# Moving one batch's rounding ahead of the first attention slots, and context and weight pieces from VectorE to GpSimd

## The reference

```python
def _fp8_linear_pertensor(x, wq, w_scale, in_scale):
    xq = _div_clamp_fp8(x, in_scale)          # divide, clip to 448, bf16, round to fp8
    return einsum('bsi,oi->bso', xq * in_scale, wq) * w_scale
...
ln_out = _ln(hidden_states, ln_w, ln_b)
q  = _ln(_fp8_linear_pertensor(ln_out, wq, ...))    # 16 heads of 128, 8 groups of 2
k  = _ln(_fp8_linear_pertensor(ln_out, wk, ...));  v = _fp8_linear_pertensor(ln_out, wv, ...)
core = _gqa(q, k, v)                                # softmax attention
qx = _ln(_fp8_linear_pertensor(ln_out, wqx, ...))
kx, vx = split(einsum('bsi,oi->bso', cond, w_kv_x))   # cond: the context, not rounded to fp8
xout = _gqa(qx, _ln(kx), vx)
cat = _div_clamp_fp8(concatenate([core, xout]), proj_smooth)
x = x + einsum('bsi,oi->bso', cat, wproj) * scales
x = x + _ffn(_layernorm(x))                         # gate, up, silu, down
```

## Time and profile before

| | |
|---|---|
| median of 3 runs | 1735.4 us |
| the profiled execution | 1738.57 us, span 1736.7 us |
| PE / PEld busy | 1632.1 us (94%) / 1228.0 us (71%) |
| DVE / ACT / POOL busy | 1410.2 (81%) / 1359.8 (78%) / 1089.6 us (63%) |
| chain that ended last | PE 71%, DVE 9%, ACT 7%, issue 5%, POOL 4% |
| busiest POOL group | L1131, 512 x 1166 ns, idle before it 296.3 us |

### The profile page before, as it was taken

One profiled execution on the slowest core, in us unless ns is written; L12 is line 12 of the kernel. 1 busy time (PEld: TensorE's weight loads), 2 busy tenths in 40 slices (PEclk: granted clock), 3 DMA queues, 4 the chain that ended last, 5 costly groups with the idle time before them and its releaser, 6 DMA issues.

```text
span 1736.7 us, 43799 instructions
## 1 busy us (share of the span) xinstructions
PE 1632.1 (94%) x15491; PEld 1228.0 (71%) x15776; DVE 1410.2 (81%) x3228; ACT 1359.8 (78%) x2908; POOL 1089.6 (63%) x1031
## 2 busy tenths in 40 slices
PE   1569999999999999999999999999999899999999
PEld 1447778888888888888888888888888544444444
DVE  8999999999999999999999999998779763323232
ACT  6978999999999999999999999999999622222221
POOL 1357777777787777777777777778777613121211
PEclk9969999999999999999999999999999999999999
DMA  5947788887888888788878887888999980303000
GB/s 177 223 111 127 140 154 144 148 153 147 148 149 156 147 145 152 147 148 146 151 147 149 148 159 147 145 140 151 188 187 187 196 244 22 138 8 142 4 24 25
DMA packets 663603, 241.45 MB, mean 139 GB/s; under 512 B 619488, under 2 KB 636000, under 8 KB 662880
## 3 DMA queue, kind: packets, MB, share of 16 engines
q1 hardware_dynamic: 662096, 230.20, 68.1%
q0 software_dynamic: 1296, 8.52, 2.4%
HBM read 75.15 MB, written 29.51 MB: 60 GB/s over the span
## 4 chain that ended last, share of the span: by engine, by line
PE 71%; DVE 9%; ACT 7%; issue 5%; POOL 4%; SPq 3%; DMA 2%; DVEq 0%; ACTq 0%; POOLq 0%
PE ps_pj L673 21%; PE ps_s L739 6%; PE ps_o L722 5%; PE ps_o L724 5%; PE ps_o L723 5%; PE ps_s L742 5%; PE ps_s L680 4%; PE ps_qt L692 4%; POOL local L1131 2%; PE ps_s L738 2%; PE ps_pj L811 2%; PE ps_s L825 2%; PE ps_o L811 2%; PE ps_pj L812 2%; PE ps_o L812 2%
## 5 line engine op out<-in xcount | busy, mean ns | idle before, releaser
L1131 POOL TENSOR_TENSOR local<-local 128x512 bf16<-128x512 f32 x512 | 597.1, 1166 | 296.3 <-ACT local L1035 296.0
L673 PE MATMUL ps_pj<-wide 128*128 128x256 bf16 (+1 forms) x5544 | 582.7, 254 | 4.8 <-DVE wide L1214 4.0
L673 PEld LDWEIGHTS ps_pj<-wide 128*128 128x128 bf16 x5544 | 470.1, 98 | 115.0 <-DVE wide L1214 4.4
L1032 ACT ACTIVATE local<-ps_s,neg_max 128x512 f32<-128x512 f32 x512 | 391.8, 765 | 43.7 <-DVE neg_max L1429 41.6
L1035 ACT ACTIVATE local<-ps_s,neg_max 128x512 bf16<-128x512 f32 x512 | 394.0, 770 | 0.0
L722 PE MATMUL ps_o<-v_hi,local 128*128 128x129 bf16 x2048 | 375.5, 221 | 5.7 <-DVE local L1437 3.2
L724 PE MATMUL ps_o<-v_hi,local 128*128 128x129 bf16 x2048 | 375.2, 219 | 0.0
L723 PE MATMUL ps_o<-local 128*128 128x128 bf16 x2048 | 375.1, 218 | 0.0
L1429 DVE TENSOR_REDUCE neg_max<-ps_s 128x1 f32<-128x512 f32 x512 | 344.7, 673 | 22.8 <-PE ps_s L742 22.7
L941 ACT ACTIVATE local<-ps_pj,head_rstd 128x128 f32<-128x128 f32 x756 | 242.0, 448 | 41.8 <-issue 41.7
L1106 POOL TENSOR_TENSOR head_rstd<-sq_sum,minus_half 128x3 f32<-128x3 f32 x256 | 223.4, 873 | 16.4 <-DVE sq_sum L1321 16.4
(11 more groups left out here) (133 smaller groups left out, 2623.5 us busy)
## 6 DMA issues: line engine op xcount, KB each, us to landing
quantised_heads<-local SPq DMA_DIRECT2D x128, 128.0 KB, 2.4
w_raw<-w_group SPq DMA_DIRECT2D x56, 256.0 KB, 3.2
wide<-quantised_heads SPq DMA_DIRECT2D x3, 4096.0 KB, 13.1
local<-local SPq DMA_TRANSPOSE x640, 3.2
wide<-packed_weights SPq DMA_DIRECT2D x32, 256.0 KB, 3.2
wide<-x SPq DMA_DIRECT2D x6, 1024.0 KB, 12.0
packed_weights<-w_proj POOLq DMA_DIRECT2D x4, 1024.0 KB, 15.2
wide<-quantised_heads SPq DMA_DIRECT2D x16, 256.0 KB, 3.4
```

The lines of the kernel that those rows point to most:

```text
L673: last = mm(dst[:, at:at + n], lhs, w_at(par, part, c, cross * 512 + at, n), start=(k == 0), stop=(k == len(terms) - 1))
L1032: a(p_exp[:, u % 2], ps_s[u % 2][:], ACT.Exp, bias=neg_max[:, u % 4:u % 4 + 1])
L1131: tt_(pp[:, u % PP_BUFS, 1], p_exp[:, u % 2], pp[:, u % PP_BUFS, 0], ALU.subtract)\
```

## The change

1. `LATE_FROM` is gone: all four chunks of batch 3 are now rounded by `quantise_late`, one chunk at a time in 20 steps. Eight steps are issued before group 0 (`LATE_BEFORE`), the other twelve in slots 0 to 5. The scratch is now `early_mag`, the space of `y` and `summed`, which is first written in slot 6. The two-chunk piece `quantise(8, 3, 0, 2)` and `ctx_rest(1)` leave the opening.
2. The low part of the context of batches 1, 2 and 3 is made by GpSimd in twelve pieces of 512 columns (`ctx_low`): four between the `qk_rest` of the opening, eight in slots 1, 2, 3, 4, 8, 14, 20, 26. ScalarE waits for the first four before group 0, TensorE and VectorE's `weight_lo` for their own counts.
3. ScalarE's high part of batch 3's context moves from the opening (one instruction of 2048 columns) to slots 2 to 5 (four of 512).
4. Weight chunks 6 and 7 (c = 2 and 3 of group 1) are centred and scaled by GpSimd, in the same slots, with `tensor_scalar`.

The program has the same DMAs as before.

```diff
+        early_mag = local[:, carve.at:carve.at + SETS * T]
...
-        LATE_FROM = 2
-        LATE_SLOTS = (7, 10, 13, 15, 17, 20, 23, 25, 27, 30)
-        CTX_SLOTS = (2, 3, 4, 5, 7, 12, 22, 30)
-        late_mag = home(W_FIRST + LATE_FROM * GW)([SETS * T], BF16)
+        POOL_SCALED = (6, 7)
+        LATE_BEFORE, LATE_SLOTS = 8, (0, 0, 1, 1, 1, 2, 2, 3, 3, 3, 4, 5)
+        CTX_AT = {1: (2, 2), 2: (2, 3), 3: (2, 0), 4: (2, 1), 8: (3, 0), 14: (3, 1), 20: (3, 2), 26: (3, 3)}
+        CTX_HIGH_AT = {2: 0, 3: 1, 4: 2, 5: 3}
...  (ScalarE)
+            def ctx_high(c):
+                act.wait_ge(ctx_loaded, 16 * B)
+                a(ctx_hi[B - 1][:, c], ctx_in(B - 1)[:, c], ACT.Copy).then_inc(ctx_hi_done, 1)
...
-            ctx_part(3)
             act.wait_ge(xq_done, OPENING_PIECES)
-            act.wait_ge(ctx_lo_done, CTX_DIRECT)
+            act.wait_ge(ctx_piece_done, CH)
...  (ScalarE, in a slot, behind the two exponentials)
+                    if first and slot in CTX_HIGH_AT:
+                        ctx_high(CTX_HIGH_AT[slot])
...  (GpSimd)
+            def weight_scale(c, piece, count):
+                if piece == 0:
+                    pool.wait_ge(w_step, 2 * count)
+                for h in range(SCALE_CUTS[piece], SCALE_CUTS[piece + 1]):
+                    head = raw(c)[:, h * D:(h + 1) * D]
+                    last = nc.gpsimd.tensor_scalar(head, head, w_mean[:, h:h + 1], wscale[:, 8 * c + h:8 * c + h + 1],
+                                                   ALU.subtract, ALU.mult)
+                if piece == len(SCALE_CUTS) - 2:
+                    last.then_inc(w_scaled, 1)
+            def ctx_low(b, c):
+                pool.wait_ge(ctx_hi_done, b + 1 if b < B - 1 else b + c + 1)
+                tt_(ctx_lo[b][:, c], ctx_in(b)[:, c], ctx_hi[b][:, c], ALU.subtract).then_inc(ctx_piece_done, 1)
...
             qk_rest(-2, 1, 1)
+            ctx_low(1, 0)
             qk_rest(-2, 2, 2)
-            for j in range(3):
-                qk_rest(-1, j, 3 + j)
+            ctx_low(1, 1)
+            qk_rest(-1, 0, 3)
+            ctx_low(1, 2)
+            qk_rest(-1, 1, 4)
+            ctx_low(1, 3)
+            qk_rest(-1, 2, 5)
...  (GpSimd, at the end of a slot)
+                    if first and slot in CTX_AT:
+                        ctx_low(*CTX_AT[slot])
+                    for piece in range(len(SCALE_CUTS) - 1):
+                        for n in prep_at(g, slot, f"scale{piece}"):
+                            if n in POOL_SCALED:
+                                weight_scale(n % CH, piece, n + 1)
...  (VectorE)
             quantise(7, 2, 2, 2, {3: (7,)})
-            ctx_rest(1)
-            quantise(8, 3, 0, 2)
+            for n in range(LATE_BEFORE):
+                quantise_late(*divmod(n, QUANT_STEPS + 1))
...
-                    for n, at in enumerate(CTX_SLOTS if first else ()):
-                        if slot == at:
-                            ctx_piece(CTX_DIRECT + n // CH, n % CH)
```

More of the change, by code:

```diff
@@ L250, in block_kernel @@
         ctx_lo_done = sem("ctx_lo_done")
+        ctx_piece_done = sem("ctx_piece_done")
         ln_step = sem("ln_step")
@@ L320, in block_kernel @@
         CTX_DIRECT = 2
-        LATE_FROM = 2
-        LATE_SLOTS = (7, 10, 13, 15, 17, 20, 23, 25, 27, 30)
-        CTX_SLOTS = (2, 3, 4, 5, 7, 12, 22, 30)
-        late_mag = home(W_FIRST + LATE_FROM * GW)([SETS * T], BF16)
-        def ctx_pieces(b):
-            return b + 1 if b < CTX_DIRECT else CTX_DIRECT + CH * (b - CTX_DIRECT + 1)
+        POOL_SCALED = (6, 7)
+        LATE_BEFORE, LATE_SLOTS = 8, (0, 0, 1, 1, 1, 2, 2, 3, 3, 3, 4, 5)
+        CTX_AT = {1: (2, 2), 2: (2, 3), 3: (2, 0), 4: (2, 1), 8: (3, 0), 14: (3, 1), 20: (3, 2), 26: (3, 3)}
+        CTX_HIGH_AT = {2: 0, 3: 1, 4: 2, 5: 3}
         GU_AT = G * HEADS * DM
@@ L422, in tile_place @@
             return (k // TILES + 1) % 2, k % TILES
-        OPENING_PIECES = CH + 2 * (B - 1) - 1
+        OPENING_PIECES = CH + 2 * (B - 2)
         def pieces_until(b):
-            return CH + 2 * b + (b == B - 1)
+            return CH + 2 * b + (2 if b == B - 1 else 0)
         def at_start(t):
@@ L764, in group @@
                         if first and b + 1 < B and i == TT and half == 1:
-                            pe.wait_ge(ctx_lo_done, ctx_pieces(b + 1))
+                            pe.wait_ge(ctx_piece_done, CH * (b + 1))
                         project((b + 1) % B, i, half, (g + 1) % 2 if b == B - 1 else g % 2, GROUP_TILES * g + TILES + k)
@@ L1023, in group @@
                             if n == CH and half == 0:
-                                act.wait_ge(ctx_lo_done, ctx_pieces(2))
-                            if n == CH + 2 and half == 0:
-                                act.wait_ge(xq_done, pieces_until(B - 1))
+                                act.wait_ge(ctx_piece_done, CH * 2)
                             weight_hi(n // CH % 2, n % CH, n + 1, half)
@@ L1210, in weight_lo @@
             def weight_lo(par, c, count):
+                if CH < count <= 2 * CH:
+                    dve.wait_ge(ctx_piece_done, CH * 2 + c + 1)
                 dve.wait_ge(w_hi_done, count)
@@ L1274, in quantise_late @@
             def quantise_late(c, step):
-                n = OPENING_PIECES + c - LATE_FROM
+                n = OPENING_PIECES + c
                 val = xq[B - 1][:, :, c]
-                magnitude = late_mag.rearrange("p (s t) -> p s t", s=SETS)
+                magnitude = early_mag.rearrange("p (s t) -> p s t", s=SETS)
                 dve.wait_ge(quant_step, QUANT_STEPS * n + step)
                 if step == 0:
-                    dve.wait_ge(in_scaled, CH * B)
+                    dve.wait_ge(in_scaled, CH * (B - 1) + c + 1)
                     v.tensor_scalar(val, val, FP8_MAX, -FP8_MAX, ALU.min, ALU.max).then_inc(quant_step, 1)
@@ L1284, in quantise_late @@
                     dve.wait_ge(xq_done, n)
-                    dve.wait_ge(ctx_lo_done, ctx_pieces(CTX_DIRECT))
                     dve.sem_inc(waited_dve, 1)
@@ L1312, in ctx_rest @@
                 v.tensor_tensor(ctx_lo[b][:], ctx_in(b), ctx_hi[b][:], ALU.subtract).then_inc(ctx_lo_done, 1)
-            def ctx_piece(b, c):
-                dve.wait_ge(ctx_hi_done, b + 1)
-                v.tensor_tensor(ctx_lo[b][:, c], ctx_in(b)[:, c], ctx_hi[b][:, c], ALU.subtract).then_inc(ctx_lo_done, 1)
             def head_squares(i, t):
@@ L1440, in group @@
                             .then_inc(y_done, 1)
-                    for n, at in enumerate(CTX_SLOTS if first else ()):
-                        if slot == at:
-                            ctx_piece(CTX_DIRECT + n // CH, n % CH)
                     for n, at in enumerate(LATE_SLOTS if first else ()):
                         if slot == at:
-                            quantise_late(LATE_FROM + n // (QUANT_STEPS + 1), n % (QUANT_STEPS + 1))
+                            quantise_late(*divmod(LATE_BEFORE + n, QUANT_STEPS + 1))
                     for n in prep_at(g, slot, "sums"):
@@ L1466, in group @@
                         for n in prep_at(g, slot, f"scale{piece}"):
-                            weight_scale(n % CH, piece, n + 1)
+                            if n not in POOL_SCALED:
+                                weight_scale(n % CH, piece, n + 1)
                     for n in prep_at(g, slot, "hi0"):
```

## The result

The changed kernel takes 1748.95 us (median of 4 runs, 1748.27 to 1749.82) against 1734.91 us (1733.77 to 1735.73) of the kernel before in runs beside it: a ratio of 1.0081, 95% interval 1.0068 to 1.0093. It is 14.0 us slower, where I forecast 3.4 us faster. The profiled execution has a span of 1747.7 us.

What follows compares the result with a forecast made beforehand. TensorE sets the steady pace, but VectorE bounds early group 0. Terms of +3.6 (start), -8.0 (slots 9 to 65) and +1.0 (heads) gave -3.4 us, a median of 1732.0; range for 8 in 10 1725.5 to 1738.5.

Steps and rivals of the forecast that it cites:

- I take 0.4: Chunks 6 and 7: a head on GpSimd costs 0.4 us, so 2.8 us a chunk.
- 1.0 us for both chunks with the casts together: Slots 33 and 43: ScalarE's casts waiting for GpSimd's last heads cost 1.0 us, bounds 0 and 10.8.
- The rival of the slow heads: Slots 33 and 43: heads of 1.15 us delay cast, exponential and scores by 10.8 us, giving 1741.8; chance 0.14.
- -8.0 in slots 9 to 65: Slots 9 to 65: VectorE relieved of 19 us, so TensorE's pace of 2.49 us a unit stands, gaining 8.0 us.
- I estimate 0.7 from scores to maximum: Unit 9: its maximum starts 0.7 us after its scores, at 137.2 against 133.60 before.
- whatever happens ahead of unit 9 shifts everything behind it: Behind unit 9: a delay or gain ahead of it carries through, so its 3.6 us counts in the sum.
- The opening and slots 1 to 5: Group 0's start: rounding steps and GpSimd holds put the first maximum at 111.4 and unit 5 at 128.9.
- The holds of 0.77 us a subtraction: Opening and slots 1 to 5: each GpSimd subtraction meeting a rounding step holds VectorE 0.77 us; 6.2 and 3.9 us.
- The powers of slots 2 and 4: GpSimd's powers get no price; by the lock rule for every GpSimd instruction they would add 1.7 us.
- +3.6 at unit 9: The start: unit 9's maximum comes at 137.2 against 133.60, 3.6 us later.
- The rival of the dear start: First slots: TensorE's clock falls again or all eight subtractions hold, about 3 us more, 1735.0; chance 0.28.
- GpSimd at no cost: Opening and slots 1 to 5: GpSimd's subtractions hold nothing, first maximum at 105.3, total 1722.0; chance 0.12.

Runs made afterwards that it cites:

- e12: The changed kernel with four GpSimd instructions a chunk instead of seven heads, weights of chunks 6 and 7 not right: 1746.09 us, ratio 1.0061.
- e13: The changed kernel with ScalarE's casts of chunks 6 and 7 two slots later, heads in the same bursts on GpSimd: 1743.29 us, ratio 1.0047.
- e6: The changed kernel with the GpSimd heads spread one a slot and casts in slots 33, 34, 45, 46: 1743.46 us, ratio 1.0050.
- e1: The changed kernel with the heads of chunks 6 and 7 back on VectorE: 1739.74 us, ratio 1.0022 to the kernel before.
- e9: The kernel before with chunk 4's heads one a slot in slots 7 to 13, on VectorE: 1736.57 us, ratio 1.0004.
- e11: The kernel before with chunk 4's heads one a slot in slots 7 to 13, on ScalarE: 1736.28 us, ratio 1.0004.
- e8: As e7, with the preparation of weight chunk 4 four slots later: 1737.55 us, ratio 1.0017 to the kernel before.
- e7: The changed kernel with heads back on VectorE and GpSimd's context pieces of slots 1 to 4 and 8 moved to 6 to 9 and 11: 1737.68 us, ratio 1.0012.
- R: The early rounding of batch 3 (part 1 of the change); alone on the kernel before 1737.39 us, ratio 1.0016.
- e5: The kernel before with only the early rounding of batch 3, context low parts and heads staying on VectorE: 1737.39 us, ratio 1.0016.
- R + C: Early rounding and context on GpSimd, without the heads on GpSimd, against the kernel before: 1739.74 us, ratio 1.0022.

## Why the prediction was wrong

**"I take 0.4" for a head, and "1.0 us for both chunks with the casts together": this step failed most.** A head is 0.79 us, and the term is +10.1 us (11.2 in the traces). The rival of the slow heads named the mechanism, the place (slots 33 and 43) and the point, 0.7 us, from which it takes the whole gain; I gave it 0.14. I had laid the head by its length between two rows of other operations, the product of 128x4 (0.19) and the subtraction of 128x512 (1.15). e12 shows that the operation counts as much: 384 columns of a head's `tensor_scalar` take 1.64 us, more than that subtraction of 512. That the small power has 0.85, near a head's 0.79, is a likeness of two numbers and no more. The rival's price was short too: for a head of 0.79 it gives 2 x (7 x 0.79 - 2.7) = 5.7 us, and 10.1 were measured. When no long wait for the last head is left, 4.1 (e13) and 4.7 (e6) stay. The other 6.0 come from the cast that stands in front of the exponentials, as e13 shows. How they are made up isn't measured; in the trace a stand of TensorE belongs to it (3.15 us at chunk 6), and the lower clock behind it (0.50 from 206 to 209 us, and again from 240 to 242).

**"-8.0 in slots 9 to 65": half right.** In e1, without the heads, unit 9 is +7.1 and unit 65 +2.5, so 4.6 us come back and 3.4 of the 8.0 do not. VectorE isn't full there any more (22.6 and 23.5 of 25 us in e1), so I take what is left not to be its work; no run shows whose it is. A piece of it is at 155 to 160 us, where e1's TensorE waits 0.8 us for `qk_rest` of the next batch and GpSimd is full, with a piece of the context (1.15 us) ahead of that `qk_rest`:

```profile
155.00:160.00 5.00, 4.20 (x47) 3.34 (x45) 4.72 (x12) 4.54 (x11) 5.00 (x5) 1.00 0.58 121
```

The busy share of an engine at 24.8 of 25 us told me that VectorE was one bound there, not that it was the only one: e9 to e11 show the same from the other side. Which share of the 3.4 us each other wait has stays open.

**"I estimate 0.7 from scores to maximum" at unit 9: wrong, at no cost.** The scores came when forecast (136.51, where the sum has 136.5), but the maximum stood behind three heads and the steps of head rounding; 140.07 instead of 137.2. The kernel before has the same 4.16 us from the maximum of unit 8 (129.44) to that of unit 9 (133.60), so its own trace could have told. e8 takes most of that gap away and the time does not move. So "whatever happens ahead of unit 9 shifts everything behind it" failed as well: offsets at unit 9 of +3.4 and +5.1 (e8, e7) end equal.

**The opening and slots 1 to 5: right.** The holds of 0.77 us a subtraction gave both positions within 0.4 us, and the lengthened steps bear the sum out; four subtractions taken away bring only 0.5 each (e7). The powers of slots 2 and 4, which I had left without a price, held no step: beside them L1313 takes 0.68 us and L1324 1.21, their usual lengths. That R makes the start late by itself (+8.7 at unit 5 in e5), with all twenty steps ahead of unit 5 on an engine that is full, the sum had too, as +3.6 at unit 9. The rival of the dear start is seen in part. The clock of 0.51 from 112 to 117 us isn't its mark, for the kernel before has 0.50 there. But TensorE then stands for 3.25 of the 4 us from 118 to 122, and the clock falls a second time:

```profile
118.00:122.00 4.00, 0.75 (x12) 0.53 (x10) 3.81 (x6) 1.58 (x3) 2.37 (x4) 1.00 0.34 66
124.00:127.00 3.00, 2.56 (x17) 1.68 (x16) 3.00 (x6) 1.78 (x3) 2.04 (x2) 0.50 0.64 93
```

In the kernel before TensorE is busy throughout, and its clock is 1.00 from 124 to 127 us as well:

```profile
118.00:122.00 4.00, 4.00 (x52) 3.35 (x51) 3.32 (x8) 2.94 (x6) 2.25 (x2) 1.00 0.86 72
```

e5 has the second fall too (0.50 from 122 to 124 us), e7 hasn't. What it costs isn't measured by itself: unit 5 came when forecast all the same. R + C ends at +3.9, where this rival had -0.4.

**GpSimd at no cost: fell** in the opening already.

No version is faster than the kernel before by more than the error: the best is the context alone, 0.9993 (0.9984 to 1.0002).

## What to carry to other kernels

Work moved to an engine with idle time costs by when it is done, not by how much idle time there is: look for the first instruction on another engine that waits for its last piece, and for what is queued behind that one (here a cast ahead of the exponentials, 6 of 10 us). An operation that no row shows can't be priced by its length between rows of other operations; time it once, or let the range reach over both rows (here 0.19 to 1.15 us, and the gain was gone at 0.7). And an engine that is full over a stretch is one bound of it; before its relief is booked as gain, look for the next wait in the same slots.
